# A four-layer cross-attention kernel: the weightings of layers one and two as pairs of 64x128 row tiles, the first layer's on the whole array, the mask moved into the copies, another prologue and another GpSimd order

## The reference

```python
# layer 0: channels are the tokens; softmax over 256 positions
A = softmax(Mn^T Mm);  x = Wo (A-weighted Ml) + bo + x      # Mn, Mm, Ml: 64x64 maps of inorm(x), inorm(ctx), ctx
# layers 1 and 2: 16 heads of 16 features
K, V = layer_norm(ctx) @ Wk.T, layer_norm(ctx) @ Wv.T
scores = Q @ K.T * 16 ** -0.5, masked per context row
x = x + tanh(gate) * (softmax(scores) @ V) @ Wo.T
# layer 3: one head of 256 features
x = x + alpha * (softmax(x @ wq.T @ (ctx @ wk.T).T / 16) @ (ctx @ wv.T)) @ wo.T
```

## Time and profile before

| | us |
|---|---|
| median of 3 runs (733.35 to 734.37) | 733.74 |
| the profiled execution's own time | 732.05 |
| its span, first to last instruction | 730.2 |
| PE busy in the span | 651.7 (89%) |
| DVE busy | 531.0 (73%) |
| ACT busy | 470.5 (64%) |
| POOL busy | 200.7 (27%) |

### The profile page before, as it was taken

The page is one execution under the profiler, slowest core; times in us unless marked ns, Lnnn a source line. Parts: engine busy times, 40 slices in busy tenths (PEclk is TensorE's granted clock), DMA queues, the critical chain, the costliest instruction groups (busy, mean ns, idle before and its releaser), DMA issues.

```text
span 730.2 us, 21782 instructions
## 1 busy us (share of the span) xinstructions
PE 651.7 (89%) x8642; PEld 585.2 (80%) x8642; DVE 531.0 (73%) x1116; ACT 470.5 (64%) x941; POOL 200.7 (27%) x169
## 2 busy tenths in 40 slices
PE   1589899988999989998999889999899989998985
PEld 1478789877998789887898779987898878987984
DVE  4977758786786858877587867868588775876664
ACT  1488675775849657586757758496575867577571
POOL 3615800146005530058001460055300580012000
PEclk9999999999999999999999999999999999999998
DMA  5310000200002000110002000020001100000000
GB/s 139 126 62 3 3 1 3 92 2 2 2 25 70 2 2 2 41 53 2 1 3 92 2 2 2 27 67 2 2 2 42 52 2 1 3 31 2 2 2 30
DMA packets 18869, 18.19 MB, mean 25 GB/s; under 512 B 2206, under 2 KB 18718, under 8 KB 18782
## 3 DMA queue, kind: packets, MB, share of 16 engines
q1 hardware_dynamic: 16854, 15.38, 6.5%
q10 hardware_dynamic: 1608, 1.18, 0.6%
q0 software_dynamic: 320, 0.27, 0.2%
HBM read 12.63 MB, written 4.19 MB: 23 GB/s over the span
## 4 chain that ended last, share of the span: by engine, by line
PE 67%; ACT 13%; DVE 8%; issue 7%; SPq 2%; DMA 1%; ACTq 0%; POOL 0%; DVEq 0%
PE psum L341 10%; PE psum L538 9%; PE psum L613 8%; PE psum L342 8%; PE psum L343 8%; ACT work L731 5%; ACT work L714 5%; PE psum L558 5%; DVE state_lo L819 5%; PE psum L421 4%; PE psum L548 2%; PE psum L416 2%; PE psum L454 2%; PE psum L425 2%; PE psum L604 2%
## 5 line engine op out<-in xcount | busy, mean ns | idle before, releaser
L1072 POOL TENSOR_TENSOR kbd<-k_tmp,own_row 128x1024 f32<-128x1024 f32 x32 | 60.7, 1907 | 377.7 <-ACT k_tmp L670 377.7
L731 ACT ACTIVATE work<-psum 128x512 f32<-128x512 f32 (+1 forms) x208 | 111.3, 590 | 58.9 <-PE psum L558 45.0
L877 DVE TENSOR_REDUCE negmax<-psum 128x8 f32<-128x512 f32 x128 | 87.6, 684 | 69.8 <-PE psum L538 69.6
L720 ACT ACTIVATE work<-shifted 128x512 f32<-128x512 f32 x128 | 79.6, 631 | 21.0 <-DVE shifted L881 20.9
L881 DVE TENSOR_TENSOR shifted<-psum,negmax 128x512 f32<-128x512 f32 x128 | 88.5, 691 | 5.4
L613 PEld LDWEIGHTS psum<-v,work 128*64 128x64 f32 x2048 | 65.4, 138 | 22.9 <-issue 19.2
L613 PE MATMUL psum<-v,work 128*64 128x34 f32 x2048 | 72.1, 225 | 12.1 <-ACT work L731 12.1
L538 PE MATMUL psum<-kbd,work 64*128 64x128 f32 x1024 | 74.0, 284 | 3.6 <-issue 3.1
L538 PEld LDWEIGHTS psum<-kbd,work 64*128 64x128 f32 x1024 | 62.6, 187 | 11.4 <-issue 10.0
L714 ACT ACTIVATE work<-psum,negmax 128x256 f32<-128x256 f32 x128 | 51.2, 512 | 26.1 <-DVE negmax L873 26.1
L558 PE MATMUL psum<-const,work 64*128 64x64 f32 x1536 | 66.5, 226 | 1.5 <-ACT work L720 1.2
(11 more groups left out here) (175 smaller groups left out, 1693.0 us busy)
## 6 DMA issues: line engine op xcount, KB each, us to landing
x_raw<-in_x_dram SPq DMA_DIRECT2D x8, 512.0 KB, 4.7
c_raw<-in_ctx_dram SPq DMA_DIRECT2D x8, 512.0 KB, 6.1
out_dram<-attn SPq DMA_DIRECT2D x16, 256.0 KB, 2.2
mrow_u<-in_mask_dram SPq DMA_DIRECT2D x8, 64.0 KB, 3.8
scratch<-in_L_xattn_ln_beta_dram POOLq DMA_DIRECT2D x2, 128.0 KB, 5.5
work<-in_L_xattn_Wq_dram ACTq DMA_DIRECT2D x1, 256.0 KB, 7.7
work<-in_L_xattn_Wk_dram ACTq DMA_DIRECT2D x1, 256.0 KB, 5.1
work<-in_L_xattn_Wv_dram ACTq DMA_DIRECT2D x1, 256.0 KB, 7.2
```

Source lines behind the costliest of these rows:

```text
L720: act.activation(e, shifted[:, i % 2, :].rearrange("t (c k) -> t c k", c=NK), ACT.Exp).then_inc(exps, 1)
L731: act.activation(probsT[:, slot, 0:width], o[:, 0:width], ACT.Copy).then_inc(free, 1)
L877: dve.tensor_reduce(negmax[:, i % 2, :], sv, AX_X, ALU.max, negate=True).then_inc(rowmax, 1)
L1072: pool.tensor_tensor(kbd[l - 1][:, i], k_tmp[:, i, :].rearrange("p (b s) -> p b s", s=C).unsqueeze(2).broadcast_to(each), own_row[:].unsqu ...
```

## The change

- **Weightings, layers one and two.** Each of the 8 pairs is now two matmuls of 64 rows by 128 columns (a batch each, both heads of a pair of heads), still 34 columns streamed, that write two banks. `v2` loses its zeros: half the size, its last column a constant one. DVE reads two banks: 2 reciprocals and 4 products of 64x128 for 1 and 1 of 128x256.
- **Weightings, layer zero.** 4 matmuls of 128x128 that stream 65 columns, for 8 of 128x64.
- **Mask.** It is the scale of ACT's copy of the transposes (`group_mask`, set once a group). A `V1` or `V2` step is one copy; DVE's mask columns go.
- **Banks.** A weighting of layers one and two takes two, so the rotation changes; the list of steps is another.
- **GpSimd.** Both key spreads come before `front` and the normalisation.
- **Prologue.** The small biases come as rows and are turned on PE with the mask (`MT`); the group is loaded first; layer one's weights move from ACT's queue to SP's; the normalisation moves from DVE to ACT; the order is another; the wait for all banks ahead of the loop goes.

```diff
-    o += S(0, 0) + S(0, 1) + S(0, 2) + S(0, 3) + X(0, 0) + X(0, 1) + p("V1", 0) + X(0, 2) + X(0, 3) + copied("V1", 0)
-    o += p("K1", 0) + T(0, 0) + T(0, 1) + S(0, 4) + S(0, 5) + X(0, 4) + T(0, 2) + T(0, 3) + X(0, 5) + p("K1", 1) + S(0, 6)
+    o += S(0, 0) + S(0, 1) + X(0, 0) + X(0, 1) + S(0, 2) + S(0, 3) + p("V1", 0) + X(0, 2) + X(0, 3) + copied("V1", 0)
+    o += p("V1", 1) + T(0, 0) + T(0, 1) + S(0, 4) + S(0, 5) + T(0, 2) + T(0, 3) + S(0, 6) + S(0, 7) + X(0, 4) + p("K1", 0)
...
+        turned = [probsT[:, 2 * n:2 * n + 2, :].rearrange("k a b -> k (a b)").rearrange("k (n c) -> k n c", c=P) for n in range(2)]
...
-        v2 = [sb(f"v2_{l}", [P, NP, NH, 2, VW]) for l in (1, 2)]
+        v2 = [sb(f"v2_{l}", [P, NP, NH, VW]) for l in (1, 2)]
...
+            load_group(0)
             sp.dma_start(const[:], cst).then_inc(const_loaded, 16)
...
-            for i, n in enumerate(("bn", "bm", "bl")):
-                sp.dma_start(w0_cols[:, i:i + 1], w[f"L0_xattn_{n}"].unsqueeze(1).unsqueeze(0).broadcast_to([2, C, 1])).then_inc(b0_loaded, 16)
-            sp.dma_start(bo_row, w["L0_xattn_bo"].unsqueeze(0).broadcast_to([P, C])).then_inc(b0_loaded, 16)
+            for n in "qkvo":
+                sp.dma_start(raw[n + "1"][:], w_in(w[f"L1_xattn_W{n}"])).then_inc(w1_loaded, 16)
+            sp.dma_start(bo_row, w["L0_xattn_bo"].unsqueeze(0).broadcast_to([P, C])).then_inc(bo_loaded, 16)
...
                         for s in range(2):
-                            for q in range(2):
-                                t0 = D * (i % 2) + P * s + C * u
-                                mm_ = pe.matmul(o[C * q:C * q + C, cols], probsT[:, (i & 2) + q, t0:t0 + C], v0[:, i, s, :],
-                                                start=s == 0, stop=s == 1)
+                            mm_ = pe.matmul(o[:, cols], turned[i // 2 % 2][:, 4 * (i % 2) + 2 * s + u, :], v0[:, i, s, :],
+                                            start=s == 0, stop=s == 1)
...
                 for j in range(NJ):
-                    for q in range(2):
-                        mm_ = pe.matmul(o[C * q:C * q + C, 2 * VW * j:2 * VW * (j + 1)], probsT[:, 2 * (i % 2) + q, C * j:C * j + C],
-                                        v2[l - 1][:, i, 2 * j + q].rearrange("k b v -> k (b v)"), start=True, stop=True)
-                mm_.then_inc(signal, 1)
+                    for to, done, rows in ((o, signal, slice(0, C)), (o2, signal2, slice(C, 2 * C))):
+                        mm_ = pe.matmul(to[:, 2 * VW * j:2 * VW * (j + 1)], turned[i % 2][rows, j, :],
+                                        v2[l - 1][rows, i, 2 * j:2 * j + 2, :].rearrange("k q v -> k (q v)"), start=True, stop=True)
...
-                    for q in range(2):
-                        for h in range(2):
-                            rows = slice(C * h, C * h + C)
-                            ins = act.activation(v2[int(name[1]) - 1][rows, 2 * i + q, :, h, 0:HD],
...
+                    act.activation(v2[int(name[1]) - 1][:, 2 * i:2 * i + 2, :, 0:HD],
+                                   o[:].rearrange("k (q n v) -> k q n v", q=2, n=NH), ACT.Copy).then_inc(free, 1)
...
+                        act.activation(dst, src, ACT.Copy, scale=group_mask[:, i:i + 1]).then_inc(free, 1)
...
-                dve.tensor_tensor(attn[:, i].rearrange("t h j d -> t j h d"), sums[:, :, :, 0:HD],
-                                  rz.unsqueeze(3).broadcast_to([P, NJ, 2, HD]), ALU.mult).then_inc(free, 1)
+                for h in range(2):
+                    for q in range(2):
+                        rows = slice(C * q, C * q + C)
+                        ins = dve.tensor_tensor(attn[rows, i, h], sums[h][rows, :, q, 0:HD],
+                                                rz[h][rows, :, q].unsqueeze(2).broadcast_to([C, NJ, HD]), ALU.mult)
+                    ins.then_inc(banks[h][1], 1)
...
             with pool.Fori(0, NG - 1) as g:
                 spread_keys(g, 1, False)
+                spread_keys(g, 2, False)
                 front(g)
-                spread_keys(g, 2, False)
+                normalise(g)
```

More of the change, by code:

```diff
@@ L396, in proj_step @@
                 if name in ("AT1", "AT2"):
-                    used = [("A", int(name[2]), 2 * i + q) for q in range(2)]
+                    used = [("A", int(name[2]), 2 * i + q, c) for q in range(2) for c in range(2)]
                 if g is None and name in ("Mn", "Mm", "V0"):
                     used = [("P", "W0" if name == "V0" else "W0T", 0)]
-                o, signal = start_fill(g, step, last, consumed=used, front=fronts("nT") if name == "K1" and i == 0 else ())
+                o, signal = start_fill(g, step, last, consumed=used, front=fronts("nT") if name in ("K1", "V1") and i == 0 else ())
+                if g is None and i == 0 and name in ("xT", "cT", "V0"):
+                    pe.wait_ge(group_loaded, 48)
                 if name == "xT":
-                    if i == 0 and g is None:
-                        pe.wait_ge(group_loaded, 48)
-                    elif i == 0:
+                    if g is not None and i == 0:
                         pe.wait_ge(group_loaded, g * 48 + 96)
@@ L590, in weighted_step @@
                     front = fronts("V0")
-                first = step if l or i % 2 == 0 else ("A", 0, i - 1)
-                if first == step:
-                    o, signal = start_fill(g, step, last, consumed=used, front=front)
-                else:
-                    wait_banks(g, last, None, consumed=used)
-                    bk, _ = fill(g, first, last)
-                    o, signal = psum[bk], full[bk]
-                if l == 0:
+                if l == 0:
+                    first = ("A", 0, i & ~1)
+                    if first == step:
+                        o, signal = start_fill(g, step, last, consumed=used, front=front)
+                    else:
+                        bk, _ = fill(g, first, last)
+                        o, signal = psum[bk], full[bk]
                     for u in range(2):
@@ L634, in _ @@
                     weight_step(step)
-            for bk in range(8):
-                pe.wait_ge(freed[bk], released(bk, PRO_FILLS[bk]))
-            pe.wait_ge(cleared, 1)
             with nc.Fori(0, NG - 1, engines=[pe.engine], hint_back_edge=True) as g:
@@ L762, in iteration @@
                         proj_step(g, ("P",) + step[1:], last)
+                    elif step[0] == "SC":
+                        set_mask(g)
                     elif step[0] == "H":
@@ L768, in iteration, with normalise_rows @@
                         turn_step(g, step, last)
+            def normalise_rows(part):
+                act.wait_ge(norm_bias_ready, 1)
+                if part:
+                    act.wait_ge(mix_ready, 1)
+                src, dst = ((x_raw, x_norm), (c_raw, c_norm))[part]
+                for n in range(NP):
+                    t = NP * part + n
+                    ins = act.activation(dst[:, n, :], src[:, n, :], ACT.Identity, scale=rstd[:, t:t + 1], bias=norm_bias[:, t:t + 1])
+                ins.then_inc(normed if part else x_normed, 1)
             def row_sum(terms, total, scale=1.0):
@@ L790, in _ @@
                 elif step[0] == "P":
+                    if step[1] == "Wk1":
+                        act.wait_ge(scales_loaded, 9 * 16)
                     weight_step(step)
@@ L808, in _, with filled @@
         def _(dve):
-            def filled(g, step, last):
-                bk, n = fill(g, step, last)
+            def filled(g, step, last, c=0):
+                bk, n = fill(g, step, last, c)
                 dve.wait_ge(full[bk], n)
@@ L1126, in _ @@
             front(None)
+            deviations(1)
             pool.wait_ge(scales_loaded, 9 * 16)
```

197 lines of the change are left out of this document (106 added, 91 removed).

## The result

| | before | after |
|---|---|---|
| median of the runs | 733.55 us | 782.26 us (780.57 to 784.3) |
| span of the profiled execution | 730.2 us | 778.8 us |
| start of the first group's scores | 48.27 us | 49.23 us |
| a group without a half-clock stretch | 84.7 us | 89.7 us |
| mean granted clock | 0.988 | 0.982 |

The change makes the kernel slower: 1.0668 times the time before, 95% interval 1.0634 to 1.0701. The forecast was 774 us, with a range of 746 to 806.

What follows compares the result with a forecast made beforehand. PE, busy 89% of the span, was taken to bound the kernel. 732.05 + 8 x (8.8 of PE work - 2.5 of waits) - 2 clock - 8 prologue = 772.5 us, with 1.7 for the median 774; range 746 to 806.

Steps and rivals of the forecast that it cites:

- PE's steps and modes: PE in the loop: weightings of layers one and two +5.9 us, layer zero +2.9, modes 0; +8.8 us a group.
- waits: PE's waits in the loop: 4.5 us go, 2 new ones come; -2.5 us a group, between -5 and +1.5.
- clock: Loop: two half-clock stretches behind the 2.1 us wait for `state_lo` go, 1 us each, -2 us in all.
- prologue: Before the first scores: bias columns leave SP's queue, DVE loses clearing and normalisation; -8 us, between 0 and -13.
- The weightings' pace: PE's weightings: 128-column loads set the pace; 16 pairs at 0.112 us, 1.80 a step; layer zero 8 records at 0.111, 0.89.
- Rival 1: PE's weightings: loads are hidden, a weighting takes about 1.0 us, layer zero's 0.47; kernel faster, 684 us; chance 0.09.
- the bound of 800 us: Whole kernel: upper end of the bounds by the forecast's own terms, 752 to 800 us.
- third rival: Layers one and two: DVE sets the pace or normalisation holds `state_lo`; waits +1.5 instead of -2.5, 806 us; chance 0.13.
- new waits: PE in the loop: DVE's 1 us more between a layer's last weighting and the transposition behind it; 2 us a group.
- The cause that I gave for `state_lo`: Loop: two POOL key spreads running beside the copy make it 3.38 us; moved ahead of `front`, 0.7 expected.
- five marks: Weightings 1.7 to 1.9 us, layer zero 0.9, `state_lo` at most 1.3, PE busy 88 with waits 3, first scores at 40.
- Rival 2: Loop and prologue: all of PE's waits go (5 us a group) and the prologue gains 13; 749 us; chance 0.13.

Runs made afterwards that it cites:

- e3_stream2: The changed kernel with twice the streamed columns (68 for 34) in the weightings of layers one and two, same loads: 773.74 us.
- e2_quads: The changed kernel with weightings of layers one and two as 64x64 tiles, each matmul split into two of 64 loaded and 17 streamed columns: 721.7 us.
- e5_after_oldpool: The changed kernel with GpSimd's old order, layer two's key spreads behind mask product and normalisation: 787.94 us.
- e4_before_pool: The kernel before with only GpSimd's new order in the loop, both key spreads ahead of mask product and normalisation: 715.16 us.
- e12_hold: The changed kernel with SyncE issuing the weights of layers one to three only once layer zero's have landed: 775.08 us.

## Why the prediction was right, and where it was not

The direction and the main term were right, the time 8 us too low. That it is only 8 is in part luck: the clock, the prologue and the last group came out some 18 us worse than forecast, and the waits 10 us better. By its own steps, span against span (730.2 to 778.8, +48.6 us):

| step | predicted | measured |
|---|---|---|
| PE's steps and modes, 8 groups | +70.4 | about +70 (5.8 and 2.9 a group) |
| waits, 8 groups | -20 | about -30 |
| clock | -2 | about +5 |
| last group beyond this | 0 | +2.5 |
| prologue | -8 | +1.0 |

- **The weightings' pace** (0.112 and 0.111 us): measured 0.112 and 0.111 to 0.112, the steps 1.78 us for 1.80 and four in 3.49 us for 3.56. The choice near the upper bound, because the scores' load is this load, held, and `e3_stream2` shows the reason: doubling the streamed columns costs nothing. Rival 1, loads hidden behind matmuls in the other tile, is out; the transposes' 0.59 us for eight pairs didn't carry over, and why a transpose's load is faster stays open. TensorEngine Tiling (Array Packing) of the Trainium skill, Overview and Key Properties, promises up to twice the throughput for two tiles side by side; a pair of 64x128 tiles does take the time of one whole-array record here (112 ns for 111). But the kernel before had two tiles side by side already, with half the columns to load (66 ns a pair); four tiles of 64x64 gain more in `e2_quads`.
- **A reading.** The prologue's row taken as two matmuls of 0.14 us each is one fp32 matmul in its two records. And the bound of 800 us doesn't come out of its terms: waits at +1.5 give 806, as in the third rival.
- **Waits.** A clean group grew by 5.0 us. With 8.7 of PE, 3.7 went, for the 2.5 taken and the 5 of the bound; modes, set at 0, are in this number and weren't separated from it. PE's idle time, 5.6 to 2.0, says the same. Of the 2 us of new waits a group 1.6 came, but more of the old ones went. The cause that I gave for `state_lo` was wrong in part: the spreads start 0.55 us behind it even in GpSimd's old order, and the new one saves only another 0.5 us (`e5_after_oldpool`). That the normalisation doesn't hold VectorE was right in this kernel (0.69 us beside it) and nearly so in `e4_before_pool` (up to 0.93). By the rule in the GPSIMD Engine Reference of the Trainium skill, Specifications, read as if it held for one-input work too, the 2.1 us would have stayed; they went.
- **Clock.** "Two in the loop, 1 us each" of the old stretches did go, but groups one to seven now stand 7.6 us above seven clean ones (two stretches in the first, one in each second), where they stood 2.5 above before. I had tied the stretches to the 2.1 us wait and not asked what PE's own work does to the clock. Of the terms of the sum, this one and the prologue failed.
- **Prologue.** The failing step is "SP's queue no longer has the columns of biases ahead of the weights (5.26 us for the last)", taken as a delay that goes. The delay did go: the last weight of SyncE's queue lands at 22.53 us for 25.96. But it had been a shield: while SyncE sat in those issues, from 3.38 to 11.55 us, it issued no weights, and layer one's stood behind layer zero's on ScalarE's queue. Now layer one's four, 1 MB, are issued by 7.83 us, and layer zero's last weight landed 8.9 us later. `e12_hold` puts an explicit wait there and brings the scores 5.9 us forward, and the time down by 7.2. I costed the removed issues and not what was issued into their place, which the change's own list of DMAs would have told. The normalisation moved to ScalarE, which I had priced at nothing, stands in the chain with 4.05 us; no run takes it out by itself, so its share isn't shown.
- **What would show it.** Of the five marks four came: 1.78 us, 0.87 a weighting of layer zero, `state_lo` at 0.69, PE busy 88.03 of 90, with waits of 2.0 where about 3 were said. The first scores at about 40 us didn't: 49.23.
- **Rivals 2 and 3.** Rival 2 wanted 20 us more from the waits and 5 from the prologue; the waits gave 10 and the prologue nothing. Against rival 3, VectorE has 67 of 90 us (about 71 of 91 were forecast), and only 0.7 us of PE's wait in a group hangs on it.

## What to carry to other kernels

Count loaded columns before streamed ones: where a matmul streamed fewer columns than it loaded (34 or 65 for 128), the larger tile was slower, and splitting its loads over column tiles gave the time back even with twice the instructions. A slow issue at a queue's head may hold back traffic that would hurt: before removing it, add up the bytes that it lets forward, and if need be keep the hold as a wait. An order that frees a collision is worth what it is worth in that list of steps; here the same edit gave 2.0 us a group in one kernel and 0.5 in the other. It may only move the collision to another instruction, so look at every copy of the group afterwards and not only at the one that was long.

## What was unexpected of the hardware

- TensorE's clock fell to half behind work without a gap: busy 3.50 of 3.50 us, then 0.53 of full clock in the next 3.4. The same steps with 68 streamed columns for 34, and the same duration, didn't make it fall (773.74 us for 782.26). From the second group on, the fall comes in every second one only. Which property of the stream decides isn't shown.
- Four 64x64 tiles take a record every 16 ns, half of what two column tiles of 128x64 take (2.02 us for 64 records, 32 ns).
- A DMA of bias rows, 1.5 KB in all, issued by 14.7 us, landed at 22.4, behind 128 KB of its own queue and the megabytes of another.
- GpSimd's one-input normalisation and VectorE's two-input copy together: in the changed kernel VectorE is unchanged at 0.69 us and GpSimd's four take 5.15 us for 4.83; in `e4_before_pool` VectorE takes 0.90 to 0.93 us and GpSimd's are unchanged. What decides which side pays isn't shown; in both the cost is 0.2 to 0.3 us, where two-input work of GpSimd cost VectorE 2.7.
- Transposes of 128 loaded columns start a pair of row tiles every 63 ns, where matmuls with as many loaded columns take 112.
